# Cross attention with spread weight splits and one-chunk affinities, and expert FFN with tokens on partitions

## The reference

```
x = layernorm(x + self_attention(x))
x = layernorm(x + cross_attention(x, ctx, ctx))
aff = x @ centroids.T;  e = argmax(aff);  alpha = sigmoid(aff[e])       # one expert a token
h  = relu((layernorm(x) * g[e] + b[e]) @ w1[e].T + b1[e])               # 256 -> 1024
ye = x + h @ w2[e].T + b2[e]                                            # 1024 -> 256
x = layernorm(x + alpha * ye + (1 - alpha) * x)
```

## Time and profile before

| what | us |
|---|---|
| median of three | 1029.28 |
| profiled execution | 1030.96 |
| its span | 1029.1 |
| mean granted clock of PE | 0.947 |
| PE / DVE / ACT / POOL busy | 930.2 / 696.1 / 745.3 / 300.5 |
| PE, DVE, ACT, POOL busy, 776 to 1009 | 222.72 / 184.65 / 166.91 / 101.14 of 233.00 |

### The profile page before, as it was taken

The page is one execution under the profiler, slowest core; times in us unless marked ns, Lnnn a source line. Parts: engine busy times, 40 slices in busy tenths (PEclk is TensorE's granted clock), DMA queues, the critical chain, the costliest instruction groups (busy, mean ns, idle before and its releaser), DMA issues. The chain is left out here.

```text
span 1029.1 us, 17730 instructions
## 1 busy us (share of the span) xinstructions
PE 930.2 (90%) x5301; PEld 513.2 (50%) x5301; DVE 696.1 (68%) x1836; ACT 745.3 (72%) x1414; POOL 300.5 (29%) x349
## 2 busy tenths in 40 slices
PE   5599999999999999999999998996179999999992
PEld 2134444444444433333333333332169998998991
DVE  5367777887778777265575664585447887787783
ACT  1488878787878869898899985893046766866861
POOL 4042314041322112002122222123333444443443
PEclk9699999999999989999999996997579999999996
DMA  8988689959696786696696684551262543453450
GB/s 218 208 224 225 154 223 262 230 175 210 195 230 171 198 219 119 155 261 108 149 186 134 132 159 86 125 119 42 70 227 105 179 178 115 158 205 124 164 216 31
DMA packets 74844, 172.04 MB, mean 167 GB/s; under 512 B 16657, under 2 KB 36039, under 8 KB 64712
## 3 DMA queue, kind: packets, MB, share of 16 engines
q1 hardware_dynamic: 67944, 156.36, 59.9%
q0 software_dynamic: 6496, 14.16, 4.0%
q10 hardware_dynamic: 320, 0.52, 0.2%
HBM read 122.23 MB, written 53.73 MB: 171 GB/s over the span
## 5 line engine op out<-in xcount | busy, mean ns | idle before, releaser
L773 ACT ACTIVATE probs<-sc 128x512 f32<-128x512 f32 x1024 | 530.3, 609 | 123.4 <-DVE sc L864 83.9
L508 PE MATMUL sc<-qst,kst 57*128 57x512 f32 (+1 forms) x1024 | 262.1, 474 | 14.6 <-DMA qst<-s_qk 12.7
L864 DVE TENSOR_TENSOR sc<-sc,strip 128x308 f32<-128x308 f32 (+1 forms) x512 | 192.0, 429 | 100.1 <-PE sc L508 98.8
L520 PE MATMUL ot<-probs,vals 128*32 128x512 f32 x1600 | 214.0, 607 | 0.1
L508 PEld LDWEIGHTS sc<-qst,kst 57*128 57x128 f32 (+1 forms) x1024 | 117.8, 188 | 177.9 <-ACT probs L773 132.6
L1735 ACT ACTIVATE f_h<-f_h_ps,par 128x384 f32<-128x384 f32 x104 | 60.8, 586 | 32.0 <-PE f_h_ps L1645 32.0
L1812 DVE TENSOR_TENSOR f_h_lo<-f_h,f_h_hi 128x384 fp32r<-128x384 f32 x104 | 66.5, 639 | 13.7 <-DVE f_h_hi L1810 5.7
L1893 POOL DMA_INDIRECT home<-s_x,get_ids x45 | 53.2, 1183 | 75.0 <-issue 42.6
L1810 DVE CAST f_h_hi<-f_h 128x384 fp32r<-128x384 f32 x104 | 37.0, 356 | 41.2 <-ACT f_h L1735 41.0
L520 PE MATMUL ms<-probs,vals 128*32 128x512 f32 x448 | 62.9, 637 | 0.0
L1906 POOL DMA_INDIRECT out<-f_normed,f_put_ids x39 | 43.0, 1103 | 64.6 <-ACT f_normed L1769 56.2
(11 more groups left out here) (189 smaller groups left out, 1619.5 us busy)
## 6 DMA issues: line engine op xcount, KB each, us to landing
s_qk<-w_hi SPq DMA_DIRECT2D x32, 512.0 KB, 7.1
strip<-in_w_all SPq DMA_DIRECT2D x16, 1024.0 KB, 7.9
f_raw<-in_w_all SPq DMA_DIRECT2D x14, 1024.0 KB, 6.7
s_x<-x SPq DMA_DIRECT2D x8, 1026.0 KB, 10.4
kst<-s_qk SPq DMA_DIRECT2D x32, 256.0 KB, 6.0
qst<-s_qk SPq DMA_DIRECT2D x32, 256.0 KB, 7.0
s_x_parts<-split SPq DMA_DIRECT2D x16, 512.0 KB, 3.1
kst<-s_ctx_parts SPq DMA_DIRECT2D x32, 256.0 KB, 6.1
```

The costliest lines, as they stand in the source:

```text
L508: nc.tensor.matmul(sc[j][:], kst[at:at + rows, i, P * c:P * c + P], qst[at:at + rows, i, :], start=True, stop=True).then_inc(scored, 1)
L520: last = nc.tensor.matmul(sums_bank(n, g)[32 * j:32 * j + 32, :], vals[:, c, 4 * g + j, :], probs[:, k % KEPT, j, :], start=(c == 0), stop ...
L773: nc.scalar.activation(probs[:, k % KEPT, j, :], sc[j][:], ACT.Exp, scale=scale).then_inc(exped, 1)
L864: nc.vector.tensor_tensor(sc[j][:, lo:hi], sc[j][:, lo:hi], band_backwards(rank_of(4 * g + j), at, hi - lo), ALU.add).then_inc(biased, 1)
```

## The change

Cross attention:

- The first expert's weights are split in bodies 3 to 5: casts in body 3 (k 1 and 15), four subtractions of half the size in bodies 4 and 5 (k 1 and 15).
- The affinities take one chunk a block, k = 12 to 15; turning x2 is one block earlier. Choosing and the gate are done at k = 0 of the body after, counting at its k = 1, the places at k = 2. `choose` and the gate stand apart (`keep_gate`). The last body does its part at k 13 to 15.
- The store of x2 stands ahead of the context's load and waits for the normalised rows also.

Experts:

- `ffn2` has the tokens on partitions: for each of three chunks of tokens, 3 matmuls of 256 columns. Its last three f are done in the next tile's first three. h has 3 banks of PSUM instead of 4, y has 3.
- ACT takes the relu twice from PSUM, once as the high half; DVE's cast is gone.
- `keep_y`, `turn_out`, `gate_rows` are gone. DVE adds y × alpha straight from PSUM to the kept rows; POOL prepares these as 2 x + alpha b2, with b2 as rows by a new DMA of 128 KB a tile.
- The normalising goes from ACT to DVE; `turn_in`, `scale_in` and `low_in` are done in two halves; `inverse_deviation` stands ahead of `keep_rows`, and the drain of `finish` is gone.

```diff
-        SPLIT_AT = B - 3
+        SPLIT_AT = B - 5
...
             def store_x2(c):
                 sp.wait_ge(weighed, c + 1)
+                sp.wait_ge(have_hat, c + 1)
...
-                if k in (13, 14):
-                    affinities(c, k - 13)
-                if k == 15:
+                if c < B - 2 and k >= 12:
+                    affinities(c, k - 12)
...
+                    if c > 1 and k == 0:
+                        choose(c - 2)
+                        keep_gate(c - 2)
...
+                    if c > 1 and k == 2:
+                        give_places(c - 2)
...
-                    if c == SPLIT_AT and k in (1, 8, 10, 11):
-                        split_w0((1, 8, 10, 11).index(k))
+                    if c == SPLIT_AT and k in (1, 15):
+                        high_w0(k // 15)
+                    if c in (SPLIT_AT + 1, SPLIT_AT + 2) and k in (1, 15):
+                        low_w0(c - SPLIT_AT - 1, k // 15)
...
             def ffn2(i, s, f):
...
                 pe.wait_ge(h_ready, FC * i + f + 1)
...
+                for t in range(TC):
+                    some = slice(P * t, P * t + P)
+                    if f == 0:
+                        wait(pe, have_res, TC * (i - 1) + t + 1)
+                    for n, (x, w) in enumerate(((h_hi, w_hi), (h_hi, w_lo), (h_lo, w_hi))):
+                        last = nc.tensor.matmul(y_ps[t][:], x[at][:, some], w[s][:, 1, col],
                                                 start=(f == 0 and n == 0), stop=(f == FC - 1 and n == 2))
...
             def step(i, s, n):
                 for f in range(FC):
                     ffn1(i, s, f)
                     if f >= LAG:
                         ffn2(i, s, f - LAG)
-                    if f == 1 and later(i):
-                        turn_out(i - 1)
-                    if f == 4:
-                        turn_in(i + 1, 1 - s, n + s)
+                    elif later(i):
+                        ffn2(i - 1, 1 - s, FC - LAG + f)
+                    if f in (3, 5):
+                        turn_in(i + 1, 1 - s, n + s, f // 5)
...
-                nc.scalar.activation(h[f % (LAG + 1)][:], h_ps[f % (LAG + 1)][:], ACT.Relu, bias=bias).then_inc(h_full, 1)
+                nc.scalar.activation(h_hi[at][:], h_ps[f % H_BANKS][:], ACT.Relu, bias=bias).then_inc(h_hi_ready, 1)
+                nc.scalar.activation(h[at][:], h_ps[f % H_BANKS][:], ACT.Relu, bias=bias).then_inc(h_full, 1)
...
-                nc.vector.tensor_copy(h_hi[at][:], h[at][:]).then_inc(h_hi_ready, 1)
...
+            def add_rows(i, s, t):
...
+                dve.wait_ge(y_done, TC * i + t + 1)
+                nc.vector.scalar_tensor_tensor(out=res[:, t, :], in0=y_ps[t][:], scalar=gate[s][:, t:t + 1],
+                                               in1=keep[s][:, t, :], op0=ALU.mult, op1=ALU.add).then_inc(have_res, 1)
...
-                nc.gpsimd.tensor_copy(keep[s][:], rows[s][:, :, 0:C + 1]).then_inc(kept, 1)
+                wait(pool, ld_b2[s], 16 * (n + 1), pool_passed)
+                nc.gpsimd.tensor_copy(gate[s][:], rows[s][:, :, C]).then_inc(have_gate, 1)
+                wait(pool, have_gate, i + 1, pool_passed)
+                for t in range(TC):
+                    nc.gpsimd.tensor_scalar(keep[s][:, t, :], b2[s][:], gate[s][:, t:t + 1], None, ALU.mult).then_inc(gated_b2, 1)
+                wait(pool, gated_b2, TC * (i + 1), pool_passed)
+                nc.gpsimd.tensor_tensor(keep[s][:], keep[s][:], rows[s][:, :, 0:C], ALU.add).then_inc(added_once, 1)
+                wait(pool, added_once, i + 1, pool_passed)
+                nc.gpsimd.tensor_tensor(keep[s][:], keep[s][:], rows[s][:, :, 0:C], ALU.add).then_inc(kept, 1)
...
             def finish(i):
-                pool.drain()
...
                 gather(i + 2, s, n + 1)
+                if later(i):
+                    inverse_deviation(i - 1)
                 keep_rows(i + 1, 1 - s, n + s)
                 if later(i):
-                    inverse_deviation(i - 1)
                     scatter_rows(i - 1)
```

More of the change, by code:

```diff
@@ L1064, in test_sums, with low_w0 @@
+            def low_w0(m, part):
+                some = slice(F * part, F * part + F)
+                dve.wait_ge(w0_hi_ready, m + 1)
+                for i in range(2):
+                    dve.wait_ge(st_xp[i], 16 * B)
+                nc.vector.tensor_tensor(w_lo0[:, m, some], raw0[:, m, some], w_hi0[:, m, some].bitcast(F32), ALU.subtract).then_inc(w0_lo_ready, 1)
             def test_sums(number_of_test, groups, least, most):
@@ L1650, in ffn2 @@
                 if f == 0:
-                    wait(pe, have_y, i)
                     wait(pe, w_hi_ready, HALVES * i)
@@ L1693, in step, with turn_in @@
+            def turn_in(i, s, n, d):
+                if d == 0:
+                    pe.wait_ge(gathered[s], 16 * TC * (n + 1))
+                wait(pe, xn_hi_ready, DC * i + d)
+                at = C + 1 + P * d
+                for t in range(TC):
+                    last = nc.tensor.transpose(turn_ps[d][:, P * t:P * t + P], rows[s][:, t, at:at + P], ident[:])
+                last.then_inc(in_mm, 1)
             def step(i, s, n):
@@ L1733, in relu @@
                 wait(act, h_ready, FC * i + f - LAG)
-                bias = par[s][:, 2 * DC + f:2 * DC + f + 1]
-                nc.scalar.activation(h[f % (LAG + 1)][:], h_ps[f % (LAG + 1)][:], ACT.Relu, bias=bias).then_inc(h_full, 1)
-            def keep_y(i, s):
-                act.wait_ge(y_mm, FC * (i + 1))
-                wait(act, out_mm, 2 * i)
-                for d in range(DC):
-                    last = nc.scalar.activation(y[:, d, :], y_ps[d][:], ACT.Identity, bias=par[s][:, 2 * DC + FC + d:2 * DC + FC + d + 1])
-                last.then_inc(have_y, 1)
@@ L1880, in finish @@
                     hat_last(i - 1, t)
-            low_in(0, 0)
+            for d in range(DC):
+                low_in(0, 0, d)
             tiles(dve, step, finish)
```

351 lines of the change are left out of this document (162 added, 189 removed).

## The result

The changed kernel takes **1037.62 us** (median of 6 runs, 1033.67 to 1039.02) against 1029.6 for the kernel before in the same runs: a ratio of 1.0069, 95% interval 1.0042 to 1.0096. The profiled execution has a span of 1036.0 us where the one before had 1029.1. Six runs of one kernel spread over 5 us, so the ratios are taken first and the parts of the sum from the traces.

What follows compares the result with a forecast made beforehand. Bounds: PE plus DVE's late deliveries in the expert tiles, ACT's exponentials in cross attention. From the profiled 1030.96 us, −11.2 − 2.4 − 1.8 + 2.4 + 5.6 − 6.0 gave 1017.6, less 1.68 to the median: 1016 us, range 998 to 1034.

Steps and rivals of the forecast that it cites:

- Cross attention: Attention up to POOL's first gather of the experts: 15.4 us less, from the moved split, affinities and attention's end.
- The split's 11.1: Cross attention: full-width weight splits leave body 5 and return as smaller pieces, removing 11.2 us of lengthened bodies.
- the small matmuls: Cross attention: affinity matmuls half absorbed by PE, 0.4 us less a body over six bodies, −2.4 us.
- the attention's end: Tail of the cross attention: choosing, gate and x2's store moved, so it ends earlier, −1.8 us.
- PE's own time: Expert tile: PE alone takes 17.75 us without the transposes back of y; 18.45 with a 0.7 us stall.
- The period with the lock: Expert tiles: POOL's additions hold DVE's two-input instructions; period 19.9 us, middle of 19.0 and 20.85, +5.6 over twelve.
- The step that failed: Expert stage: PE busy 222.72 of 233.00 us at granted clock 1.00, so only fewer columns or stalls shorten a tile.
- The tail: Kernel's end: POOL's drain and the last turning of y go, −6.0 us, between 3.5 and 8.6 saved.
- First tile: First expert tile: keep_rows holding the port +1.4 us, three banks for h instead of four +1.0, sum +2.4.
- Rival C: Expert stage: POOL becomes the bound, late scatters and gathers delay PE, 22 us a tile, 1041 us; chance 0.22.
- D: Cross attention: split pieces and gate still stall bodies 3 to 5, its 15.4 us not returned, 1024 or 1031; chance 0.12.
- B: Expert stage: the lock costs little, POOL finds DVE's gaps, period 18.5 us, 999 us in all; chance 0.26.

Runs made afterwards that it cites:

- The filled stall: Changed kernel with eleven extra 384-column matmuls on PE ahead of each tile's first wait for low_in; 1025.01 us, ratio 0.9899 to the kernel before.
- keep_copy: Changed kernel with keep_rows only copying alpha and x, the doubling of x and alpha b2 left out; 1008.76 us, ratio 0.9758 to the kernel before.
- the kernels with fillers: Changed kernel with POOL's doubling and alpha b2 replaced by ten memsets (1033.71 us, ratio 1.0007) or seven three-column powers (1039.75 us, ratio 1.0043).

## Why the prediction was wrong

It forecast −13 us and the median moved by +8, outside the range and on the other side.

- **Cross attention: right.** −13.9 for −15.4. The split's 11.1 came whole, the small matmuls and the rest of the bodies gave 1.8 where 2.4 was said, and the attention's end 1.7 where 1.8 was said. The rest is the 0.8 by which the first exponential starts later.
- **PE's own time: right.** 17.75 worked out, 17.86 measured; 18.45 with low_in behind low_w, 18.42 measured with POOL's arithmetic out.
- **The period with the lock: the mechanism right, the working half luck.** 19.9 was said, 19.97 is what a tile takes at the full clock. But I had the multiplications of POOL at 0.40 us, from a copy, and they are 0.95 in the median and 1.06 in the mean; and I split the difference over the second addition, where it is the first one, pushed late by these multiplications, that holds low_in.
- **The step that failed:** "There is no more clock to win there; a tile gets shorter only by fewer PE columns or fewer PE stalls", with the new stall priced at its length and its effect on the clock at nothing. In half of the tiles a stall of 2.1 us or more also costs 3.3 us and more at half the clock behind it. That is 21.02 − 19.97 = 1.05 us a period in the mean, 11.5 us over eleven: 10.2 of them the clock, 1.3 the longer stalls of the first tiles. It is the largest term missed. The earlier trace rows has the granted clock at 1.00 for the stage before; I read it as nothing to win and did not ask what the new stall would lose, though the first tile of the same trace has the clock at 0.50 behind a stall of 2.77. The filled stall shows it.
- **The tail: wrong,** the second term missed, by 4.9 us. −6.0 was the drain's idle. It is paid at the program's end instead; −1.1 measured. A stall of 1.64 us before the last f of the second matmul is a low_h held for 1.99 us by POOL's addition for a tile that never runs.
- **First tile: +2.4 in the sum, but by luck.** `keep_copy` has its first tile at 20.37, so POOL's arithmetic is worth 2.8 there where 1.4 was said, and the rest is −0.4 where 1.0 was said for the three banks of h. The clock is part of both: from the first `ffn1` on it is at half for 7.8 us before, 4.2 after and 5.9 in `keep_copy`, so the terms can't be told apart better. The first gather to the first ffn1 took 1.1 more, which was not in the sum.
- **Slips** that change nothing: 82.80 − 71.68 is 11.1, and 8 × 2.13 + 0.74 is 17.78; no row shows the 0.09 of refill. The low_h of 1.72 us starts at 862.92, before POOL's copy does (863.38 to 864.21), and ends 0.4 after it, so it is a weaker witness for the hold than the prediction has it.

Rival C gave 1041 us and came nearest to the time, but its reason did not hold for this kernel: POOL waits for DVE, not DVE for POOL. It is true of the kernels with fillers and with keep_rows behind the scatters, where a chain longer by 1.5 to 3.4 us than the 19.1 of the changed kernel was the bound. D did not happen. B's period of 18.5 is what the expert part has once POOL's arithmetic is gone; its 999 us is not, since B kept the −6.0 of the tail.

Not settled: why only some of the equal stalls bring the clock down, and what POOL waits for at the program's end. In the changed kernel the hold was not separated from POOL's length by equal lengths, since both fillers ran long; it rests on the timeline, where low_in starts at 868.45 and ends 0.4 us after the addition, on POOL's waits for DVE, and on the kernel in which low_in alone was moved.
